# Attention and FFN block on one core: matrix engine's score banks shared in two rotations, weighted values in pairs

## The reference

```python
attn = jnp.einsum('bhqd,bhkd->bhqk', q, k) / scale
attn = attn + slopes[None, :, None, None] * dist[None, None, :, :]
attn = jax.nn.softmax(attn, axis=-1)
out = jnp.einsum('bhqk,bhkd->bhqd', attn, v)
...
h = jax.nn.silu(_tlin(x, w1_w, w1_s)) * _tlin(x, w2_w, w2_s)
h = jax.nn.gelu(_tlin(h, h1_w, h1_s), approximate=False)
h = jax.nn.gelu(_tlin(h, h2_w, h2_s), approximate=False)
return _tlin(h, w3_w, w3_s)
```

## Time and profile before

| | before |
|---|---|
| median of 3 runs | 879.19 us (879.15 to 880.36) |
| the profiled execution's own time | 880.13 us |
| its span | 878.3 us |
| PE busy | 814.5 us (93%) |
| DVE busy | 639.1 us (73%) |
| ACT busy | 621.6 us (71%) |
| POOL busy | 315.8 us (36%) |
| mean share of the DMA engines, 200 to 300 us | 0.59 |

### The profile page before, as it was taken

How to read it: one execution, slowest core, us unless ns; L and a number is a source line. 1 busy time by engine, 2 the same in 40 slices (tenths; PEclk the granted TensorE clock), 3 DMA queues, 4 the chain that set the end, 5 groups by cost and what they waited for, 6 DMA issues and landing times. The chain is left out here.

```text
span 878.3 us, 22823 instructions
## 1 busy us (share of the span) xinstructions
PE 814.5 (93%) x8322; PEld 578.9 (66%) x8322; DVE 639.1 (73%) x1300; ACT 621.6 (71%) x1093; POOL 315.8 (36%) x491
## 2 busy tenths in 40 slices
PE   1599999999999999999999859999999999999994
PEld 1366666666666666666666537888888888888873
DVE  4578888787878787878788445677777777777774
ACT  4067777777777777777777727777777777777772
POOL 7455555555555555555564520000100000000001
PEclk9999999999999999999999969999999999999998
DMA  4775656555656555555664201011111111111001
GB/s 134 151 164 136 139 146 140 147 145 128 140 143 157 128 149 128 147 130 147 141 146 82 63 20 31 24 37 36 36 36 37 36 36 36 36 36 36 25 24 49
DMA packets 101950, 81.22 MB, mean 92 GB/s; under 512 B 11808, under 2 KB 94880, under 8 KB 101856
## 3 DMA queue, kind: packets, MB, share of 16 engines
q1 hardware_dynamic: 100976, 77.05, 35.8%
q0 software_dynamic: 880, 2.88, 1.4%
HBM read 45.82 MB, written 33.55 MB: 90 GB/s over the span
## 5 line engine op out<-in xcount | busy, mean ns | idle before, releaser
L656 DVE TENSOR_REDUCE negmax<-ps_a 128x2 f32<-128x512 f32 x512 | 327.8, 683 | 73.1 <-PE ps_a L411 69.6
L584 ACT ACTIVATE probs<-ps_b 128x512 f32<-128x512 f32 x512 | 281.1, 596 | 59.0 <-PE ps_b L411 57.6
L396 PE MATMUL ps_a<-qk_stack 52*128 52x256 bf16 x1024 | 192.6, 278 | 31.5 <-DMA qk_stack<-qk_scratch 18.2
L404 PE MATMUL ps_b<-qk_stack 54*128 54x256 bf16 x1024 | 187.0, 274 | 0.7 <-ACT probs L584 0.7
L922 ACT ACTIVATE gelu_f<-ps_r,sc 128x512 f32<-128x512 f32 x128 | 88.3, 690 | 79.8 <-PE ps_r L863 72.3
L411 PE MATMUL ps_a<-corner_sb,eye_sb 64*128 64x128 bf16 x1024 | 141.7, 220 | 0.0
L411 PE MATMUL ps_b<-corner_sb,eye_sb 64*128 64x128 bf16 x1024 | 138.6, 216 | 0.6 <-issue 0.6
L454 PE MATMUL ps_o<-probs,v_aug 128*32 128x256 f32 x2048 | 137.0, 385 | 0.0
L396 PEld LDWEIGHTS ps_a<-qk_stack 52*128 52x128 bf16 x1024 | 64.2, 95 | 101.9 <-issue 54.7
L1020 POOL TENSOR_SCALAR vareps_f<-meanvar_f 128x4 f32<-128x4 f32 x16 | 5.7, 354 | 334.9 <-DVE meanvar_f L1006 334.9
L860 PE MATMUL ps_r<-g1h,h_hi 128*128 128x512 f32 x256 | 102.8, 401 | 1.9 <-DVE g1l L987 1.9
(11 more groups left out here) (101 smaller groups left out, 1465.7 us busy)
## 6 DMA issues: line engine op xcount, KB each, us to landing
qk_stack<-qk_scratch SPq DMA_DIRECT2D x64, 384.0 KB, 5.8
qk_scratch<-qk_sb SPq DMA_DIRECT2D x64, 192.0 KB, 2.5
qk_scratch<-qk_sb SPq DMA_DIRECT2D x96, 128.0 KB, 2.5
xT_sb<-in_xT SPq DMA_DIRECT2D x32, 128.0 KB, 2.2
qk_stack<-mrow SPq DMA_DIRECT2D x256, 2.0 KB
x_sb<-in_x SPq DMA_DIRECT2D x32, 128.0 KB, 2.6
x_scratch<-x_sb SPq DMA_DIRECT2D x32, 128.0 KB, 2.0
x_in<-x_scratch SPq DMA_DIRECT2D x32, 128.0 KB, 2.1
```

What stands on the lines that cost most here:

```text
L396: pe.matmul(ps_a[a_bank(k)][:, qb * SEQ:(qb + 1) * SEQ], q_stack[i][rows_of, j, qb * P:(qb + 1) * P], k_stack[i][rows_of, j, :], start=(qb ...
L404: pe.matmul(ps_b[B_BANK[k]][:, kb * SEQ:(kb + 1) * SEQ], k_stack[i][rows_of, j, kb * P:(kb + 1) * P], q_stack[i][rows_of, j, :], start=(kb ...
L584: nc.scalar.activation(probs[:, h % HALF, :], ps_b[B_BANK[k]][:], ACT.Exp, scale=slope[h]).then_inc(exp_done, 1)
L656: nc.vector.tensor_reduce(negmax[:, h_a // HALF, h_a % GROUPS, h_a % HALF // GROUPS, :], ps_a[a_bank(k)][:].rearrange("p (b k) -> p b k", ...
```

## The change

**Banks.** `ps_m` is gone; `ps_b` has four banks instead of three. The small work joins the rotations of the scores: `wo` and `turn o`, which DVE reads, take the next bank of `ps_a`; v, both maxima transposes, `turn norm` and qk, which ACT reads, take the next bank of `ps_b`. So per step 18 uses rotate over three banks of `ps_a`, and 21 over four banks of `ps_b`. `take_a` and `take_b` wait for the reader of the bank's use before.

**Weighted values.** Groups 2 and 3 of batch t - 1 both stand in slot 3, groups 0 and 1 of batch t both in slot 9 (`AT`). `probs` has sixteen heads, and ACT's exponentials wait for two groups further back.

**Places.** `max 0` goes from slot 6 to 5, `turn o` from 4 to 5, `turn norm` from 8 to 7. `max 1`, qk, v and `wo` stay. DVE's normalisation goes from slot 4 to 5, its statistics one slot later. ACT's copy of `max 0` goes from slot 6 to 5. ACT's copy of `ps_o` stays in slot 2. No matmul, activation or DMA is added or removed.

```diff
-PV_AT = (6, 10, 14, 2)
-SMALL_AT = {"v": 0, "turn o": 4, "turn norm": 8, "qk": 12}
+AT = {"v": 0, "wo": 0, "pv 2": 3, "pv 3": 3, "turn o": 5, "max 0": 5, "turn norm": 7, "pv 0": 9, "pv 1": 9, "qk": 12, "max 1": 14}
 AHEAD = 4
 STACKS = 4
-B_BANK = (0, 1, 2, 0, 1, 2, 0, 2, 1, 0, 2, 1, 0, 2, 1, 2)
-A_USES = [*range(7), "max 0", *range(7, 15), "max 1", 15]
-A_BANKS = 3
+A_USES = [use for k in range(HEADS) for use in (k, *(n for n in ("wo", "turn o") if AT[n] == k))]
+B_USES = [use for k in range(HEADS) for use in (k, *(n for n in ("v", "max 0", "max 1", "turn norm", "qk") if AT[n] == k))]
+A_BANKS, B_BANKS = 3, 4
...
-def b_released(t, k):
-
-    before = [g for g in range(k - HEADS, k) if B_BANK[g % HEADS] == B_BANK[k]][-1]
-    return t * HEADS + before + 1
...
-def a_bank(use):
-
-    return A_USES.index(use) % A_BANKS
-
-
-def a_before(t, use):
-
-    at = A_USES.index(use) - A_BANKS
-    return t + at // len(A_USES), A_USES[at % len(A_USES)]
...
+def a_bank(t, use):
+
+    return (t * len(A_USES) + A_USES.index(use)) % A_BANKS
+
+
+def b_bank(t, use):
+
+    return (t * len(B_USES) + B_USES.index(use)) % B_BANKS
+
+
+def a_batch(t, use):
+
+    return t - {"wo": 2, "turn o": 1}[use] if isinstance(use, str) else a_slot(t, use)[0]
+
+
+def b_batch(t, use):
+
+    return t + {"v": 0, "max 0": 1, "max 1": 1, "turn norm": -1, "qk": 4}[use] if isinstance(use, str) else t
+
+
+def last_use(t, use, uses, banks, batch, first):
+
+    at = t * len(uses) + uses.index(use) - banks
+    while at >= first * len(uses):
+        t, n = divmod(at, len(uses))
+        if live(batch(t, uses[n]), BATCH):
+            return t, uses[n]
+        at -= banks
+    return None
...
-        probs = sb("probs", [P, HALF, BLK * SEQ])
+        probs = sb("probs", [P, HEADS, BLK * SEQ])
...
-        ps_b = [ctx.enter_context(nc.psum_tensor(f"ps_b{i}", [P, 512], F32)) for i in range(3)]
+        ps_b = [ctx.enter_context(nc.psum_tensor(f"ps_b{i}", [P, 512], F32)) for i in range(B_BANKS)]
-        ps_m = ctx.enter_context(nc.psum_tensor("ps_m", [P, 512], F32))
...
+            def take_a(t, use):
+
+                before = last_use(t, use, A_USES, A_BANKS, a_batch, FIRST)
+                if before is not None:
+                    b = a_batch(*before)
+                    if before[1] == "wo":
+                        wait(pe, res_done, b + 1)
+                    elif before[1] == "turn o":
+                        wait(pe, normed, b + 1)
+                    else:
+                        wait(pe, max_done, b * HEADS + a_slot(*before)[1] + 1)
+                return ps_a[a_bank(t, use)]
+
+            def take_b(t, use):
+
+                before = last_use(t, use, B_USES, B_BANKS, b_batch, FIRST)
+                if before is not None:
+                    b = b_batch(*before)
+                    if before[1] == "v":
+                        wait(pe, v_copied, b + 1)
+                    elif before[1] == "turn norm":
+                        wait(pe, oT_copied, b + 1)
+                    elif before[1] == "qk":
+                        wait(pe, qk_copied, b + 1)
+                    elif isinstance(before[1], str):
+                        wait(pe, m_copied, b * 2 + int(before[1][-1]) + 1)
+                    else:
+                        wait(pe, exp_done, b * HEADS + before[1] + 1)
+                return ps_b[b_bank(t, use)]
...
-                    wait_a(t, k)
+                    to_a = take_a(t, k)
-                    wait(pe, exp_done, b_released(t, k))
+                    to_b = take_b(t, k)
...
             def turn_max(t, hf):
-                use = f"max {hf}"
-                wait_a(t, use)
                 wait(pe, max_done, (t + 1) * HEADS + (hf + 1) * HALF)
-                pe.transpose(ps_a[a_bank(use)][0:BLK * HALF, 0:P], negmax[:, hf, :, :, :].rearrange("p g h a -> p (g h a)"),
+                ps = take_b(t, f"max {hf}")
...
             def project_out(t):
-                if live(t + 3, BATCH):
-                    wait(pe, qk_copied, t + 4)
                 wait(pe, oT_copied, t - 1)
+                ps = take_a(t, "wo")
...
             def turn_o(t):
-                if live(t, BATCH):
-                    wait(pe, v_copied, t + 1)
-                wait(pe, res_done, t - 1)
                 wait(pe, o_copied, t)
+                ps = take_a(t, "turn o")
...
-                    if k == SMALL_AT["v"]:
-                        if live(t, BATCH):
-                            project_v(t)
-                        if live(t - 2, BATCH):
-                            project_out(t)
-                    if k == SMALL_AT["turn o"] and live(t - 1, BATCH):
+                    if k == AT["v"] and live(t, BATCH):
+                        project_v(t)
+                    if k == AT["wo"] and live(t - 2, BATCH):
+                        project_out(t)
+                    if k == AT["max 0"] and live(t + 1, BATCH):
+                        turn_max(t, 0)
+                    if k == AT["max 1"] and live(t + 1, BATCH):
+                        turn_max(t, 1)
+                    if k == AT["turn o"] and live(t - 1, BATCH):
                         turn_o(t)
-                    if k == SMALL_AT["turn norm"] and live(t - 1, BATCH):
+                    if k == AT["turn norm"] and live(t - 1, BATCH):
                         turn_norm(t)
-                    if k == SMALL_AT["qk"] and live(t + 4, BATCH):
+                    if k == AT["qk"] and live(t + 4, BATCH):
                         project_qk(t)
-                    if k == PV_AT[3] and live(t - 1, BATCH):
-                        pv(t - 1, 1 - par, 3)
-                    if k in PV_AT[:3] and live(t, BATCH):
-                        pv(t, par, PV_AT.index(k))
-                    if k == PV_AT[0] and live(t + 1, BATCH):
-                        turn_max(t, 0)
-                    if k == PV_AT[2] and live(t + 1, BATCH):
-                        turn_max(t, 1)
+                    for j in range(2):
+                        if k == AT[f"pv {j + 2}"] and live(t - 1, BATCH):
+                            pv(t - 1, 1 - par, j + 2)
+                        if k == AT[f"pv {j}"] and live(t, BATCH):
+                            pv(t, par, j)
...
-                            wait(act, pv_done, t * 4 + k // GROUP - 1)
+                            wait(act, pv_done, t * 4 + k // GROUP - 3)
...
-                    if k == 6 and live(t + 1, BATCH):
+                    if k == 5 and live(t + 1, BATCH):
...
                     if k == 0 and live(t - 2, BATCH):
                         wait(dve, wo_done, t - 1)
-                        if live(t, BATCH):
-                            wait(dve, v_copied, t + 1)
                         wait(dve, xb_done, t - 1)
                         wait(dve, x1_done, t - 3)
-                        nc.vector.tensor_tensor(res[par][:].rearrange("p a d -> p (a d)"), ps_m[:, 0:BLK * D],
+                        nc.vector.tensor_tensor(res[par][:].rearrange("p a d -> p (a d)"),
+                                                ps_a[a_bank(t, "wo")][:, 0:BLK * D],
                                                 xb_sb[par][:].rearrange("p a d -> p (a d)"), ALU.add).then_inc(res_done, 1)
+                    if k == 1 and live(t - 2, BATCH):
                         wait(dve, res_done, t - 1)
                         for a in range(BLK):
                             nc.vector.bn_stats(bn6[:, a, :], res[par][:, a, :]).then_inc(bn_done, 1)
-                    if k == 1 and live(t - 2, BATCH):
+                    if k == 2 and live(t - 2, BATCH):
                         wait(dve, bn_done, (t - 1) * BLK)
                         for a in range(BLK):
                             nc.vector.bn_aggr(meanvar[par][:, a, :], bn6[:, a, :]).then_inc(stats_done, 1)
-                    if k == 4 and live(t - 1, BATCH):
-                        normalise(t - 1)
+                    if k == 5 and live(t - 1, BATCH):
+                        normalise(t)
```

More of the change, by code:

```diff
@@ L280, in attention @@
         FIRST, LAST = -4, BATCH + 1
+        assert all(a_bank(t, use) != 0 for t, use in ((BATCH, "wo"), (BATCH, "turn o"), (BATCH + 1, "wo")))
         pieces = []
@@ L380, in _, with score_max, score_exp @@
         def _(pe):
[L381 to L392, removed]
+            def take_a(t, use):
[24 more added lines that the diff above has]
+                return ps_b[b_bank(t, use)]
+            def score_max(ps, i, h, qb):
                 g, j = h % GROUPS, h // GROUPS
                 rows_of = slice(g * TILE, g * TILE + KA)
-                pe.matmul(ps_a[a_bank(k)][:, qb * SEQ:(qb + 1) * SEQ], q_stack[i][rows_of, j, qb * P:(qb + 1) * P],
+                pe.matmul(ps[:, qb * SEQ:(qb + 1) * SEQ], q_stack[i][rows_of, j, qb * P:(qb + 1) * P],
                           k_stack[i][rows_of, j, :], start=(qb == 0), stop=False, skip_group_check=True)
-            def score_exp(i, k, kb):
+            def score_exp(ps, i, k, kb):
                 h = k ^ 1
@@ L499, in turn_norm @@
```

(19 more changed lines are left out.)

39 lines of the change are left out of this document (17 added, 22 removed).

## The result

| | before | after |
|---|---|---|
| median | 879.62 us | 868.04 us (865.22 to 868.63) |
| ratio | | 0.9857, 95% interval 0.983 to 0.9884 |
| the profiled execution, its span | 880.13, 878.3 | 867.45, 865.7 |

One execution of the kernel after, disturbed on the chip, is left out. The kernel is 1.4% faster, 12 us; forecast were 21. The time lies in the forecast's wide range (852 to 870), not in its own one (854 to 863).

What follows compares the result with a forecast made beforehand. PE was taken to set the pace, at 14.38 us per batch. Pairs 0.26, breaks 0.09 and waits 0.29 made 0.64, taken as 0.69; over 31 batches 21.4 us, median 857.8 us, own range 854 to 863, wide range 852 to 870.

Steps and rivals of the forecast that it cites:

- The pair: Two groups of weighted values in a row on PE take 1.87 us, saving 0.13 for each of two pairs.
- my terms (2 x 0.13, two breaks of 0.09): Per batch on PE: 0.13 per pair for the change back to scores, 0.09 per break between scores.
- the estimate: Two pairs without their two tiling mode changes each, a drain of 0.05 us apiece, would save 0.21 in all.
- `turn norm`'s wait: PE waits 0.34 us at `turn norm` for DVE's product, the one wait that stays.
- The three old ones go: PE's three waits per batch, 0.31 ahead of S(7), 0.26 ahead of S(8) and 0.11 ahead of S(4), disappear.
- The walk: Blocks laid in new order from S(0) = 0, giving waits after of 0.39 against 0.68 before, gain 0.29.
- The fourth bank just covers the late copy: ACT stands 1.5 us ahead of its `ps_o` copy; four `ps_b` banks hide this, by 0.1 us at the tightest.
- Sum per batch: Pairs 0.26, fewer breaks 0.09 and waits 0.29 make 0.64; 0.69 us taken, a new batch of 13.69.
- The 0.05 on top, for rounding: Without 0.09 of rounding in the old sum the gain is 0.74; 0.69 was taken, between it and 0.64.
- Hidden by 0.2: At S(0), SP's rows of `max 0` allow a start at 13.4 us, and S(0) comes at 13.6.
- my rival of the late rows: Rows of `max 0` land over 2.2 us behind issue, after S(0) is due: at 2.5, 889 us; chance 0.06.
- 31 full batches: All but the last of 32 batches gain 0.69 us each, 21.4 us in all; start and tail keep their work.

Runs made afterwards that it cites:

- the later copy: Changed kernel with ACT's copy of `ps_o` behind the exponential of slot 3 instead of slot 2: 870.01 us, ratio 0.9906 to the kernel before.
- POOL's two versions: POOL instead of SP issues the rows of `max 0`: in the changed kernel 870.47 us; with groups 0 and 1 also apart, in steps 1 to 25, 864.11 us.
- the first pair alone: Changed kernel with groups 2 and 3 still together in slot 3, groups 0 and 1 apart in slots 6 and 10: 861.12 us, ratio 0.9776.

## Why the prediction was right, and by how much it was off

- *The pair.* Forecast 1.87, measured 1.86. Pulled apart, two pairs cost 0.49; my terms (2 x 0.13, two breaks of 0.09) give 0.44. By the Trainium skill, TensorEngine Tiling (Array Packing), Key Properties (a change of tiling mode drains the engine), and TensorE: Matmul & The Clock Gate, Part 2 (a drain is about 128 cycles), the estimate was 0.21, which the measurement more than doubles.
- *`turn norm`'s wait.* Forecast 0.34, measured 0.36, for the product, as said. "The three old ones go" holds, but a new one came, 0.20 at S(7), which takes the bank that DVE reduces just ahead of the reciprocal. The walk let the two reductions end 2 x 0.61 behind their start, at 6.25; by its own row two of them last 1.29, so 6.34. They were recorded to end at 6.42, and S(7) was due at 6.3, not 6.4, because `turn o` came sooner.
- *ACT.* "The fourth bank just covers the late copy": right, shown by three banks (+1.06 us a batch) and by the later copy (no change). What is queued on ACT behind the copy starts later, but PE did not feel it.
- *Sum per batch.* Forecast 0.69, measured 14.38 - 13.77 = 0.61 in a regular one. The sum of the parts was 0.64. The 0.05 on top, for rounding, had no ground: in the trace's nanoseconds the two kinds of score cost 0.347 and 0.422, so eight of each make 6.15 and the 6.16 of the sum stands.
- *SP's queue, the step that was mis-sized.* "Hidden by 0.2" took every issue at its usual length and the landing at 1.20. Both vary: issues of 0.4 took 1.6 and more, and S(0) started up to 2.6 us behind the issue. This was my rival of the late rows. Its mechanism came, with landings over the 2.2 that it asked for, but in single batches; in the others long issues did it. The spread is not new: steps 2 to 27 have 15 SP issues of over 1.3 us before and 17 after, and before one landing took 2.90. What is new is the margin. Before, the rows are recorded as landed 0.75 to 3.0 us ahead of S(0). The change takes 1.08 of this, 0.46 by the later copy of `max 1` and 0.62 by the shorter batch. Of 27 such margins (S(0) of steps 2 to 28) five were under 1.08, and five S(0) of the same stretch became late, not all the same ones. The forecast had read one batch of this trace. Late batches cost 4.05 us in the 26 of the profile, of which S(0) is about half, where before they cost 0.35.
- *31 full batches.* The first two steps after 48 us got 1.3 us longer instead of 1.4 shorter (0.9 longer in the other execution of the kernel after, so part is chance): step 0 takes 14.14 instead of 12.93, since S(8) waits for the first rows of `max 1` (the row below). Their issue ended at 51.23 and their landing is recorded at 55.60, 0.09 ahead of S(8); before, S(8) also stood 0.09 behind its landing, but at 54.63. The last steps, which have no qk and hold other work of DVE, gained 0.4 instead of 2.1. These two are the error in "31 of the 32 batches run in this regime".
- *The tail* gained 1.3 by luck: around the handover TensorE ran at its lower level, 1.2 GHz, for 17.1 us before and for 10.2 after (clock rows below). From the last v projection on, the traces with 10.2 us take 386.3 to 386.7 us (four), those with 17.1 take 387.6 to 388.7 (four; POOL's two versions and the pairs on the old banks are left out, since they also take longer up to the FFN). It varies between executions of one kernel (17.1 in the other one of the kernel after), so I don't count it to the change.

S(8) in step 0 after:

```profile
55.69 0.27 PE L429 MATMUL ps_a<-qk_stack 52*128 52x256 bf16 x1 [1.54 <-DVE negmax L679]
```

The windows of the handover, before and then after; (1 - 0.53) x 11 / 0.5 is 10.3 us at half clock:

```profile
506.00:524.00 18.00, 9.21 (x29) 6.90 (x30) 6.86 (x18) 6.19 (x8) 4.23 (x7) 0.61 0.09 25
524.00:528.00 4.00, 4.00 (x11) 2.59 (x11) 2.67 (x5) 0.51 (x1) 0.00 (x0) 0.60 0.00 0
```

```profile
497.00:508.00 11.00, 5.05 (x17) 3.75 (x16) 2.55 (x9) 2.67 (x4) 2.51 (x4) 0.53 0.04 15
```

Profiled, 21.4 forecast less 1.9 (regular batches), 3.7 (late ones), 2.7 (first two steps) and 1.7 (last steps), plus 1.3, is 12.7: 880.13 to 867.45.

What the forecast did not see at all is how the gain divides. The banks with the new slots and the larger `probs` bring all of it and more: 14.38 to 13.74. The pairs then save 0.35 per batch and a wait of 0.18 ahead of `max 0`, and cost 0.36 at `turn norm` and 0.20 at S(7): 13.77. And the first pair, by taking group 2 out of slot 14, starts SP's chain 1.0 us later, after which S(0) is late in one batch of five. Between the two profiled executions (867.45 and 861.25) 4.9 us lie in these 26 batches, most of it their lateness, and 2.4 in the last three steps; the tail gives 1.4 back. New banks with all groups apart (860.69) and with the first pair alone (861.12, or 861.67 one slot later) beat both kernels and can't be told apart. With the first pair alone the regular batch is shorter, but it meets SP's chain sooner.

## What to carry to other kernels

Before moving a block of matmuls, ask which other engine's work it hides: group 0 stood over DVE's normalisation, and moving it cost what pairing gained. Ask too which chain it gives time: group 2 behind `max 1` gave SP's 1.0 us. When a margin of a DMA chain is a few tenths of a microsecond, take the spread of issue and landing over all batches of the trace, not their usual values in one. Try the parts of a change apart: here one part was better than the whole.

## What the hardware showed unexpectedly

A DMA issue of SP that mostly takes 0.37 to 0.64 us sometimes takes 1.6 and more, before the change as well, at times together with a stand of PE that no semaphore explains (0.7 to 1.0 us at S(7)). These stands went when POOL issued four of the rows, but also when all groups stood apart; the cause of their coming together is not shown.

TensorE's clock can fall behind such stands. In the second execution of the kernel after, PE stood to 230.28, and the window behind it shows a granted clock of 0.83 where its neighbours have 1.00:

```profile
230.00:240.00 10.00, 9.40 (x123) 6.37 (x125) 6.48 (x15) 5.31 (x11) 4.44 (x7) 0.83 0.74 167
```

(1 - 0.83) x 10 / 0.5 = 3.4 us of it ran at the lower of the two levels, 1.2 GHz, and the batch behind the stand took 15.35 instead of 13.77. So a late landing can cost more than its own length. It need not: with the first pair alone PE was idle for longer, and the clock stayed at 1.00 in the windows before, around and behind it (280 to 290 us here):

```profile
282.23 0.27 PE L429 MATMUL ps_a<-qk_stack 52*128 52x256 bf16 x1 [1.83 <-DVE negmax L679]
```

```profile
280.00:290.00 10.00, 8.17 (x133) 5.52 (x129) 7.42 (x17) 5.91 (x14) 5.00 (x9) 1.00 0.85 179
```
